# Eight gated experts: the down products as one plain single-precision matmul each, their operands no longer split

## The reference, cut to what matters

```
logits = xt @ Wg.T;  scores = softmax(logits);  w, idx = top_k(scores, 2);  w = w / w.sum()
cw = zeros((T, E)).at[arange(T)[:, None], idx].add(w)
h   = silu(einsum('td,ehd->teh', xt, W1)) * einsum('td,ehd->teh', xt, W3)
out = einsum('teh,edh->ted', h, W2)
y   = einsum('te,ted->td', cw, out)
x   = x + tanh(g_ffn[1]) * y
```

## Time and profile before

| | |
|---|---|
| Time, median of 3 runs | 702.86 us (702.14 to 708.02) |
| The profiled execution | 703.3 us, its span 701.5 us |
| PE | 613.8 us busy, 88% of the span |
| PEld | 416.7 us, 59% |
| DVE | 506.6 us, 72% |
| ACT | 393.2 us, 56% |
| POOL | 119.5 us, 17% |
| TensorE's granted clock, mean | 0.934 of full speed |

### The profile page before, as it was taken

How to read it: one execution, slowest core, us unless ns; L and a number is a source line. 1 busy time by engine, 2 the same in 40 slices (tenths; PEclk the granted TensorE clock), 3 DMA queues, 4 the chain that set the end, 5 groups by cost and what they waited for, 6 DMA issues and landing times.

```text
span 701.5 us, 8610 instructions
## 1 busy us (share of the span) xinstructions
PE 613.8 (88%) x3265; PEld 416.7 (59%) x3271; DVE 506.6 (72%) x685; ACT 393.2 (56%) x501; POOL 119.5 (17%) x64
## 2 busy tenths in 40 slices
PE   5799999879889999976579557799998889999997
PEld 2478888458557777731136013565653665788885
DVE  4967777677367899879996865764675763687775
ACT  3188888345446656536575652442313543888884
POOL 6510000400000000035396431400004001000000
PEclk8889999999999999996885889999999999999999
DMA  6124111100007010210000000026422000341100
GB/s 225 57 96 177 60 31 64 36 29 3 1 1 273 33 36 29 61 30 1 0 1 1 0 0 1 15 69 258 135 69 89 3 1 2 99 173 60 42 20 30
DMA packets 15098, 40.52 MB, mean 58 GB/s; under 512 B 1832, under 2 KB 6184, under 8 KB 15056
## 3 DMA queue, kind: packets, MB, share of 16 engines
q1 hardware_dynamic: 15056, 39.97, 16.6%
HBM read 39.27 MB, written 0.69 MB: 57 GB/s over the span
## 4 chain that ended last, share of the span: by engine, by line
PE 69%; DVE 19%; ACT 5%; issue 3%; POOL 3%; DMA 1%; DVEq 0%; SPq 0%; ACTq 0%; POOLq 0%
PE ps L583 38%; DVE work L1148 4%; PE ps L620 4%; PE ps L468 4%; PE ps L597 2%; PE ps L437 2%; PE ps L373 2%; PE ps L493 2%; PE ps L480 2%; PE ps L599 2%; PE ps L598 2%; PE ps L559 2%; ACT work L842 2%; PE ps L360 2%; POOL work L1465 1%
## 5 line engine op out<-in xcount | busy, mean ns | idle before, releaser
L1269 DVE TENSOR_TENSOR h_lo<-h_act,h_hi 128x1024 fp32r<-128x1024 f32 (+2 forms) x116 | 116.0, 1000 | 46.7 <-ACT h_hi L884 46.6
L1438 POOL TENSOR_TENSOR rstd<-var_eps,minus_half 128x4 f32<-128x4 f32 x16 | 16.4, 1035 | 428.1 <-DVE var_eps L959 428.1
L583 PE MATMUL ps<-n_hi,w_hi 128*128 128x512 f32 (+1 forms) x232 | 82.0, 401 | 5.7 <-DVE h_act L1246 3.2
L842 ACT ACTIVATE work<-work 128x2048 f32<-128x2048 f32 x32 | 59.9, 1904 | 43.0 <-DVE work L1148 34.9
L884 ACT CAST h_hi<-h_act 128x1024 fp32r<-128x1024 f32 x68 | 71.4, 1050 | 18.2 <-PE ps L583 16.3
L583 PE MATMUL ps<-n_hi,w_lo 128*128 128x512 f32 (+1 forms) x232 | 80.6, 395 | 0.0
L583 PE MATMUL ps<-n_lo,w_hi 128*128 128x512 f32 (+1 forms) x232 | 80.6, 395 | 0.0
L559 PE MATMUL ps<-work,p_rest 128*32 128x512 f32 x256 | 44.5, 796 | 35.0 <-ACT work L842 34.7
L1465 POOL TENSOR_TENSOR work<-xc,txt 128x2048 f32<-128x2048 f32 x14 | 61.8, 4424 | 39.4 <-ACT work L842 38.7
L583 PE MATMUL ps<-h_hi,w_hi 128*128 128x512 f32 (+1 forms) x184 | 62.0, 395 | 4.6 <-DVE h_lo L1269 4.6
L583 PE MATMUL ps<-h_hi,w_lo 128*128 128x512 f32 (+1 forms) x184 | 61.2, 391 | 0.0
(11 more groups left out here) (220 smaller groups left out, 1150.9 us busy)
## 6 DMA issues: line engine op xcount, KB each, us to landing
work<-g_rows SPq DMA_DIRECT2D x38, 512.0 KB, 6.7
w_f<-in_w SPq DMA_DIRECT2D x17, 512.0 KB, 3.5
w_f<-in_w SPq DMA_DIRECT2D x8, 544.0 KB, 3.5
w_f<-in_w SPq DMA_DIRECT2D x16, 128.0 KB, 2.2
w_f<-in_w SPq DMA_DIRECT2D x16, 64.0 KB, 2.5
p_rest<-in_p_rest SPq DMA_DIRECT2D x1, 871.0 KB, 8.5
p_attn<-in_p_attn SPq DMA_DIRECT2D x1, 547.5 KB, 6.9
x<-in_xT SPq DMA_DIRECT2D x1, 512.0 KB, 3.6
```

What stands on the lines that cost most here:

```text
L583: mm = pe.matmul(dst[i], wap(wt, e, lo, size, rows), mv[i], start=(first and c == 0), stop=(last and c == 2))
L842: act.activation(tanhs[:, g % 3], sums[:, g % 3], ACT.Tanh).then_inc(x2["tanh"], 1)
L1269: dve.tensor_tensor(h_lo[at_slot], src, h_hi[at_slot].bitcast(F32), ALU.subtract).then_inc(s["lo"], 1)
```

## The change: what it does

In layer 1 alone:

- `down` is one plain single-precision matmul of `w_f32` and `h_part` (line 642 of the changed kernel), in place of three. ACT's `high`, DVE's `low` and both splits of the down weights go.
- The down product reads `w_f32` itself. So `load` of expert e waits until all downs of the expert two before it are done (`h_used`), where it waited for that expert's low parts. One expert, not two, is loaded ahead of the gate rows in SP's list.
- `hidden` reuses a slot of `h_part` once the down that read it is done, where it waited for `low`.
- The first loads of layer 2 wait for the last down of layer 1.

The core of the diff (semaphore lists and the other layers' branches are left out):

```
@@ sync: load
-                if e >= m.slots:
+                if e >= m.slots and m.layer == 1:
+                    sp.wait_ge(mo[1]["h_used"], m.n * (e - m.slots + 1))
+                elif e >= m.slots:
                     low_ready(sp, m, e - m.slots, "u")
                     low_ready(sp, m, e - m.slots, "d")
...
-                    if m.layer != 3:
+                    if m.layer == 1:
                         low_ready(sp, last, last.experts - 1, "d")
+                    if m.layer == 2:
+                        sp.wait_ge(mo[1]["h_used"], last.total)
...
-                for e in range(m.slots, 2 * m.slots):
+                early = 1 if m.layer == 1 else m.slots
+                for e in range(m.slots, m.slots + early):
                     load(m, e)
...
@@ tensor: down
-                    pe.wait_ge(s["lo"], step + 1)
-                    if k == 0:
-                        low_ready(pe, m, e, "d")
+                    if L == 1:
+                        pe.wait_ge(s["mul"], step + 1)
...
                     if m.gated:
-                        hv = [[h[0:size, (step % 4) // 2, half(step % 2)]] for h in (h_hi, h_lo)]
-                        products([ps[:, acc + k % 2]], e, m.up + ci * P, P, size, hv[0], hv[1], **ends).then_inc(s["h_used"], 1)
+                        pe.matmul(ps[:, acc + k % 2], wap(w_f32, e, m.up + ci * P, P, size), h_part[step % 4][0:size],
+                                  start=ends["first"], stop=ends["last"]).then_inc(s["h_used"], 1)
                         return
@@ scalar: hidden, and the loop of layer 1
-                        act.wait_ge(s["h_used" if L == 2 else "lo"], step - parts + 1)
+                        act.wait_ge(s["h_used"], step - parts + 1)
...
-                    for step in range(m.total + 1):
-                        if step < m.total:
-                            hidden(step)
-                        if step >= 1:
-                            high(step - 1)
+                    for step in range(m.total):
+                        hidden(step)
                         if step == 4:
                             copy_gates()
-                        next_weights(step, N, N + 3)
+                        e = (step - N) // N + m.slots
+                        if step >= N and step % N == 0 and e < m.experts:
+                            split_hi_up(m, e)
@@ vector: the loop of layer 1
-                        low(step - 1)
...
-                        next_weights(step, N + 1, N + 4)
+                        e = at_expert(step, N + 1)
+                        if e is not None and e + m.slots < m.experts:
+                            split_lo(m, e + m.slots, "u")
```

More of the change, by code:

```diff
@@ L206, in flamingo @@
         mo = [{k: sem(f"m{m.layer}_{k}") for k in ["hid", "act", "h_used", "whu", "wlu", "wlu_first"] + ["mul"] * m.gated
-              + (["scaled", "sel"] if m.layer == 2 else ["hi", "lo", "whd", "wld", "wld_first", "gate", "acc"]) + ["xn"] * (m.layer == 3)} for m in MOES]
+              + (["scaled", "sel"] if m.layer == 2 else ["gate", "acc"]) + ["hi", "lo", "whd", "wld", "wld_first"] * (not m.gated) + ["xn"] * (m.layer == 3)} for m in MOES]
         w_in = [[sem(f"w{m.layer}_in{u}") for u in range(m.slots if m.layer != 2 else 0)] for m in MOES]
@@ L338, in _ @@
                     spread(m, e)
-                for e in range(2 * m.slots, m.experts):
+                for e in range(m.slots + early, m.experts):
                     load(m, e)
@@ L621, in down @@
                         return
-                    pe.wait_ge(s["lo"], step + 1)
-                    if k == 0:
-                        low_ready(pe, m, e, "d")
+                    if L == 1:
+                        pe.wait_ge(s["mul"], step + 1)
+                    else:
+                        pe.wait_ge(s["lo"], step + 1)
+                        if k == 0:
+                            low_ready(pe, m, e, "d")
                     if k < m.gates:
@@ L775, in first_weights @@
                     split_hi_up(m, e)
-                    if m.layer != 2:
+                    if not m.gated:
                         split_hi_down(m, e)
@@ L878, in high @@
                 def high(step):
[L879 to L891, removed]
+                    sl = step % 2
+                    act.wait_ge(s["act"], step + 1)
+                    if step >= 2:
+                        act.wait_ge(s["h_used"], step - 1)
+                    act.copy(h_hi[:, sl], h_act[:, sl]).then_inc(s["hi"], 1)
                 def copy_gates():
@@ L1261, in low @@
                     dve.wait_ge(s["hi"], step + 1)
[L1262 to L1268, removed]
+                    at_slot, src = (slice(0, P), step % 2), h_act[:, step % 2]
                     dve.tensor_tensor(h_lo[at_slot], src, h_hi[at_slot].bitcast(F32), ALU.subtract).then_inc(s["lo"], 1)
@@ L1341, in moe @@
                     weigh_chosen(m)
-                    low(0)
                     for step in range(2, m.total + 1):
@@ L1448, in first_weights @@
                     o = e * m.width
-                    for part, c0, c1 in (("u", 0, m.up), ("d", m.up, m.width)):
+                    for part, c0, c1 in (("u", 0, m.up), ("d", m.up, m.width))[:1 if m.gated else 2]:
                         pool.wait_ge(s[f"wh{part}"], e + 1)
```

## The result

| | before | after |
|---|---|---|
| Median of the runs | 702.5 us (4) | 754.6 us (4: 747.4 to 756.9) |
| Ratio, with its 95% interval | | 1.0705 (1.061 to 1.080) |
| The profiled execution | 703.3 us, span 701.5 | 747.4 us, span 745.6 |
| Layer 1, first down to x done | 98.2 us | 149.8 us |
| The rest of the span | 603.3 us | 595.8 us |

The change makes the kernel 7% slower. Layer 1 runs from the first record of down(0) in the chain of waits to the end of the last piece of x: before 206.53 to 304.77, after 205.68 to 355.44.

What follows compares the result with a forecast made beforehand. TensorE's list of matmuls was taken to bound layer 1, 2.09 us a step. Terms +7.0 - 1.0 + 35.1 + 11.4 = +52.5 on 703.3 gave 755.8, stated as 755, range 746 to 766 (0.84).

Steps and rivals of the forecast that it cites:

- 44 downs: Layer 1, downs standing between ups: a plain matmul costs 0.158 us more than three split ones, +7.0 us (+6.2 to +7.6).
- End of the layer: Layer 1's last four downs no longer wait for high and low: -1.0 us (-0.7 to -1.4).
- Six bare loads: Layer 1, experts 2 to 7: nothing covers the load released by a down; 5.85 us each, +35.1 (33.3 to 39.6).
- Clock: Layer 1, behind each of six idle stretches: TensorE at half clock, 1.9 us lost each, +11.4 (8.1 to 15.6).
- The rival that dense matmuls keep the clock: Layer 1's six waits: dense matmuls precede them, so the clock does not fall; 744 us, chance 0.05.
- The step that failed: Sign of being wrong: layer 2 or anything else outside layer 1 moves by more than 2 us.
- The edit at nothing: Gate rows behind expert 2's load: no cost, since VectorE reaches expert 0's gate only after up(9), some 8 us later.
- Layer 2's first loads: Issued at layer 1's last down, 7 us before ScalarE takes them, landing 3.5: no cost; uncovered, a microsecond or two.

Runs made afterwards that it cites:

- second experiment: Changed kernel with each expert's load in two parts: up columns as early as before the change, down columns after the last down of e - 2; 712.1 us, ratio 1.009.
- the other two executions: Two more profiled executions of the changed kernel, unaltered: 754.7 and 756.9 us, with layer 1 at 150.4 and 151.8 us.
- the wait alone: Kernel before, all products split, with layer 1's loads of experts 2 to 7 also waiting for downs and one expert loaded ahead of gate rows; 749.1 us, ratio 1.060.
- TensorE kept busy: Changed kernel with 24 small matmuls, whose result nobody reads, in each of the six waits; 745.0 us, ratio to before 1.054.
- the fifth experiment: Changed kernel with weight splits of experts 2 to 7 four to five steps later and gate rows ahead of expert 2's load; 714.2 us, ratio 1.015.
- the first: Changed kernel with the up weights' splits four steps later on ScalarE and three on VectorE, load still waiting for the down; 714.8 us, ratio 1.012.

## Why the prediction was right, step by step

| Term | Predicted | Measured | Read from |
|---|---|---|---|
| 44 downs | +7.0 | +7.4 | steps of 2.2565 us (43 without a wait, second experiment) for 2.0886 (91.90 / 396 x 9) |
| End of the layer | -1.0 | -0.9 | 5.59 for 6.51 us |
| Six bare loads | +35.1 | +34.2 | TensorE's waits, 33.2, and 6 x 0.16 to count from 0.86 us behind the down's start |
| Clock | +11.4 | +10.9 | work behind the six waits |
| Sum, layer 1 | +52.5 | +51.6 | the layer itself: +51.5 |

Each term stood within its bounds. In the other two executions the same sum gives +52.2 and +53.5, where the layer shows +52.1 and +53.5. These sums must come out, since the clock's term is what the layer took beyond its steps and waits; they show that nothing was missed. That each term has the cause named is shown by experiments: the load in two parts for the downs, the wait alone for the loads, TensorE kept busy for the clock. That the forecast of 755 met the median of 754.6 so closely is luck: the four executions spread over 9.5 us. What the traces bear out is layer 1, +52.5 predicted, +51.5, +52.1 and +53.5 measured.

**The downs.** That three matmuls went and the layer had more work to do is read from starts: 0.86 us for one plain product, 0.70 for three split ones. The load in two parts shows the term alone: 6.5 us with the end included.

**The loads.** The rule that found them: the down that releases the load and the up that needs it are neighbours in TensorE's list. Nothing between them can cover a load, and the split's unchanged place in ScalarE's list, harmless with 14.6 us in hand, put silu and product on the path as well. The two experiments that undo either half agree: the wait alone costs 6.0% of the total, the change with the wait taken away 0.9%. The term came out 0.9 us smaller because silu starts 0.68 us after the split's start, not 0.78, and the six landings are 3.44 us in the mean, not 3.5.

**The clock.** All six bursts start at half, with an up of 2.92 or 2.93 us; the loss is 1.8 us a burst (10.9 / 6). The rival that dense matmuls keep the clock is refuted by these ups, and the clock's price shown by the kernel with matmuls in the wait: 9.9 us. About 0.5 us of the 10.9 is not the clock: in that kernel, at the full clock, the first up behind a wait still took some 0.09 us beyond its step. The Trainium skill, TensorE: Matmul & The Clock Gate, "HAM oscillation — how this bites in real kernels", has bursts of matmuls with a wait for a load between them start at the lower clock. This trace agrees in all six; an estimate from the Trainium skill's example there, 0.8 us a burst, is under half of the 1.8 measured here.

**The step that failed** is the last one, "if layer 2 or anything else outside layer 1 moves by more than 2 us". In the execution profiled first it moved by 7.5 us, and that says nothing of the change: two more executions of the same kernel are within 0.8 us of the kernel before's one profile there. I had taken the clock in the pair sums as a property of the work; it differs between executions of the same work. As a test the sentence had to be made on layer 1's own time, or on several executions.

**The edit at nothing that was not free** is the place of the gate rows. Under the wait for the load it cost nothing, as predicted. With that wait gone TensorE stands for 3.5 us and layer 1 takes 6.3 us more than with everything covered; in the other order it stands for 2.7 us and the layer takes 3.0 more. The margin was also smaller than predicted: the first gate row was issued 3.7 us behind expert 2's load (217.85 and 221.59), not some 2. Layer 2's first loads were covered, as predicted: issued at 353.53, with the split that needs them at 360.69, 7.2 us later as against 7.

## What to carry to other kernels

When an operand is no longer copied, its buffer is held until the last user has read it; look in the user's own list for what stands between that read and the first instruction that needs the next load, for only that can cover the load. Count a saved pass (a cast, a split, a matmul) at its price on the engine that sets the pace, and read prices from start to start: fewer matmuls need not be less time. Where a form is cheaper in latency and dearer in throughput, use it only where the pacing engine has nothing else to do, as at the ends of layers here, and look first what already runs in that pause.

## What the runs showed of the hardware that I had not expected

- The length of TensorE's pause alone did not decide when the clock fell. In the six waits it fell 2.1, 5.0, 4.8, 4.9, 4.9 and 3.2 us after the last matmul had ended, in four of them only some 0.5 us ahead of the next one. After 2.71 us without a matmul, in the fifth experiment, the up ran at the full clock (1.68 us, clock 1.00); after 3.49 us, in the first, at half (2.93 us, clock 0.50). Whether a wait half a microsecond shorter would have kept the clock was not tested. The windows of the second and the sixth wait of the changed kernel in which the clock fell (that of the first, 219 to 220, stands above):

```profile
243.00:244.00 1.00, 0.00 (x0) 0.00 (x0) 0.43 (x1) 1.00 (x3) 0.00 (x0) 0.89 0.00 0
...
325.00:326.00 1.00, 0.00 (x0) 0.00 (x0) 0.00 (x0) 0.00 (x0) 0.00 (x0) 0.85 0.26 105
```

- The time lost to the half clock goes down from wait to wait and then jumps: 3.0, 2.3, 1.8, 1.6, 1.4 and 2.9 us in the last execution, 1.6, 1.4, 3.0, 2.2, 1.7 and 1.4 in the one before it. In the kernel with the wait alone it goes up over the first five: 1.7, 2.0, 2.1, 2.2 and 2.3. The first up always takes 2.92 or 2.93; what varies is how much of the next step is slow too. Why was not tested.
- A load of 544 KB that landed in 3.2 to 3.7 us in the six waits took 7.66 us behind the eight gate rows, 4 MB on the same queue.
